# Node pass of a two-layer graph network kernel: where VectorE forms the small products in its step

## The reference

```python
h = maximum(layernorm(x), 0)
x = x + L0(h, edges)          # L0(h) = h + (edge messages summed by dst) @ Wo.T + bo
h = maximum(layernorm(x), 0)
# L1: GCN with self loops, then a two-layer head
h7  = segment_sum((h @ W)[col] * norm, row) + b     # includes the node itself: h * dinv * dinv
out = relu(h7 @ W1 + b1) @ W2 + b2
x = x + out
```

## Time and profile before

| | us |
|---|---|
| median of 3 runs | 1850.17 (1849.44 to 1851.53) |
| the profiled execution, whole | 1868.97 |
| its span, first to last instruction | 1867.3 |
| PE busy in the span | 1629.1 (87%) |
| DVE busy | 1412.2 (76%) |
| POOL busy | 1227.1 (66%) |
| ACT busy | 1119.3 (60%) |

### The profile page before, as it was taken

One profiled execution on the slowest core, in us unless ns is written; L12 is line 12 of the kernel. 1 busy time (PEld: TensorE's weight loads), 2 busy tenths in 40 slices (PEclk: granted clock), 3 DMA queues, 4 the chain that ended last, 5 costly groups with the idle time before them and its releaser, 6 DMA issues.

```text
span 1867.3 us, 29386 instructions
## 1 busy us (share of the span) xinstructions
PE 1629.1 (87%) x6406; PEld 1099.9 (59%) x6406; DVE 1412.2 (76%) x5503; ACT 1119.3 (60%) x2092; POOL 1227.1 (66%) x864
## 2 busy tenths in 40 slices
PE   8788999999999967676675169999999999999998
PEld 4355666666666635454454046666666666666666
DVE  7986777777777639777776497888888888888873
ACT  0155555556666522222222378889889889989984
POOL 3246777777777646888887765666666666666650
PEclk9999999999999987878777679999999999999999
DMA  9997666666666655555556678999999999999981
GB/s 370 419 415 244 175 175 174 174 174 175 177 177 185 195 136 115 118 111 108 113 115 126 136 200 248 255 266 271 269 268 268 267 270 267 267 268 269 274 230 75
DMA packets 148023, 398.67 MB, mean 214 GB/s; under 512 B 20144, under 2 KB 56756, under 8 KB 147974
## 3 DMA queue, kind: packets, MB, share of 16 engines
q1 hardware_dynamic: 89830, 280.18, 43.8%
q0 software_dynamic: 56416, 115.46, 32.8%
q10 hardware_dynamic: 1728, 2.50, 0.4%
HBM read 217.84 MB, written 180.23 MB: 213 GB/s over the span
## 4 chain that ended last, share of the span: by engine, by line
PE 27%; POOL 25%; issue 13%; DMA 11%; DVE 10%; ACT 7%; another core or an unknown queue 4%; SPq 3%; ACTq 0%; DVEq 0%; POOLq 0%
POOL sums_dram L488 9%; DMA out_dram<-cg 8%; PE bank L1361 6%; PE bank L1350 6%; POOL kept L578 6%; PE bank L1246 4%; POOL cg L492 4%; POOL b_rs L484 4%; ACT z L1054 4%; DVE cg L958 3%; PE bank L1178 2%; PE bank L1253 2%; PE bank L1340 2%; SPq L394 1%
## 5 line engine op out<-in xcount | busy, mean ns | idle before, releaser
L1350 PE MATMUL bank<-kept,w 128*128 128x512 f32 x784 | 355.4, 596 | 0.0
L1361 PE MATMUL bank<-w_sb,kept 128*128 128x256 f32 x1568 | 354.3, 379 | 0.0
L578 POOL TENSOR_TENSOR kept<-kept 128x1024 f32<-128x1024 f32 x98 | 232.4, 2371 | 183.4 <-DVE cg L958 183.4
L1361 PEld LDWEIGHTS bank<-w_sb,kept 128*128 128x128 f32 x1568 | 297.9, 190 | 81.9 <-issue 46.4
L488 POOL DMA_INDIRECT sums_dram<-ub,sidx x148 | 244.1, 1649 | 91.3 <-issue 42.3
L1314 PE MATMUL bank<-cg,en 128*128 128x256 f32 x386 | 132.8, 489 | 124.7 <-issue 80.6
L484 POOL TENSOR_TENSOR b_rs<-b_ve,minus_half 128x8 f32<-128x8 f32 x102 | 210.5, 2064 | 28.7 <-DVE b_ve L975 28.7
L1350 PEld LDWEIGHTS bank<-kept,w 128*128 128x128 f32 x784 | 142.6, 192 | 142.3 <-issue 142.3
L1145 ACT ACTIVATE kept<-kept,b_nb,b_rs 128x256 f32<-128x256 f32 x392 | 202.2, 588 | 21.9 <-DVE b_nb L948 21.9
L1246 PE MATMUL bank<-qkv_w,zT 128*128 128x512 f32 x392 | 192.0, 612 | 21.4 <-DVE msg L815 18.0
L1135 ACT ACTIVATE kept<-kept,b_nb,b_rs 128x256 f32<-128x256 f32 x392 | 202.2, 589 | 12.5 <-DVE b_nb L948 12.5
(11 more groups left out here) (172 smaller groups left out, 3260.3 us busy)
## 6 DMA issues: line engine op xcount, KB each, us to landing
sums_dram<-cg SPq DMA_DIRECT2D x196, 512.0 KB
kept<-in_x_dram SPq DMA_DIRECT2D x97, 512.0 KB, 5.7
kept<-sums_dram POOLq DMA_DIRECT2D x97, 512.0 KB, 9.8
cg<-sums_dram SPq DMA_DIRECT2D x97, 512.0 KB, 8.7
out_dram<-cg SPq DMA_DIRECT2D x97, 512.0 KB, 9.8
row_d<-in_dst_dram SPq DMA_DIRECT2D x49, 128.0 KB
row_k<-keys_dram SPq DMA_DIRECT2D x24, 256.0 KB
row_s<-in_src_dram SPq DMA_DIRECT2D x24, 256.0 KB
```

What stands on the lines that cost most here:

```text
L578: pool.tensor_tensor(X1[k.slot(8)], X[k.slot(4)], H[k.slot(2)], ALU.add).then_inc(g_xh, 1)
L1350: ins = pe.matmul(bank[:, 2 + m, :], w01[:, c, m * P:(m + 1) * P], hT[k.slot(2)][:, c * GN:(c + 1) * GN], start=(c == 0), stop=(c == KC - 1))
L1361: ins = pe.matmul(to, rT[k.slot(2)][:, c * GN + j * P:c * GN + (j + 1) * P], w2_sb[:, c, :], start=False, stop=(c == KC - 1), skip_group_c ...
```

## The change

DVE's two small products of step s-1 (with their wait for POOL's roots) leave the head of its step s. They go behind the statistics, aggregates and variances of step s and ahead of `AG`. No instruction is added or dropped, and no other engine's code is touched.

```diff
@@ -938,15 +938,6 @@
             def nodes(s):
                 a, v, r, t = s, s.back(1), s.back(5), s.back(4)
                 z = v.slot(2)
-                if v.within(NG + 4):
-                    dve.wait_ge(g_rs, v.value(1))
-                    if r.within(NG):
-
-                        dve.tensor_tensor(b_rs[z][:, G:2 * G, 0], b_rs[z][:, G:2 * G, 0],
-                                          dinv2[:, bass.ds(r.value(0, G), G)], ALU.mult).then_inc(g_rsd, 1)
-                        dve.wait_ge(g_rsd, r.value(1))
-                    dve.scalar_tensor_tensor(b_nb[z][:, :, :], b_mv[z][:, :, 0:1], -1.0, b_rs[z][:, :, :],
-                                             ALU.mult, ALU.mult).then_inc(g_nb, 1)
                 k = s.back(10)
                 if k.within(NG):
 
@@ -974,6 +965,15 @@
                     dve.wait_ge(g_mv, a.value(1))
                     dve.tensor_scalar(b_ve[a.slot(2)][:, :, :], b_mv[a.slot(2)][:, :, 1:2], EPS, None,
                                       ALU.add).then_inc(g_ve, 1)
+                if v.within(NG + 4):
+                    dve.wait_ge(g_rs, v.value(1))
+                    if r.within(NG):
+
+                        dve.tensor_tensor(b_rs[z][:, G:2 * G, 0], b_rs[z][:, G:2 * G, 0],
+                                          dinv2[:, bass.ds(r.value(0, G), G)], ALU.mult).then_inc(g_rsd, 1)
+                        dve.wait_ge(g_rsd, r.value(1))
+                    dve.scalar_tensor_tensor(b_nb[z][:, :, :], b_mv[z][:, :, 0:1], -1.0, b_rs[z][:, :, :],
+                                             ALU.mult, ALU.mult).then_inc(g_nb, 1)
                 k = s.back(6)
                 if k.within(NG):
                     dve.wait_ge(g_h1, k.value(1))
```

## The result

| | before | changed |
|---|---|---|
| median, us | 1850.59 (1849.44 to 1851.53) | 1964.28 (1961.99 to 1965.17) |
| ratio | 1 | 1.0617 (1.0600 to 1.0633) |
| span of the profiled execution, us | 1867.3 | 1963.5 |

The change costs 113.7 us, 6.2%. The prediction was 1937 us (+87), with a range of 1918 to 1990: the direction and the place were right, the size 27 us short. The measured time lies inside that range, but above the 1918 to 1960 us that the forecast had given itself without a rival.

The account below looks back on a forecast made before the run. PE was taken to bound the node pass at 7.76 us a group. A new loop through M1's banks (+91.7), stalls (0) and the beginning (-5) gave +86.7 us on 1850.2, so 1937 us, range 1918 to 1990.

Parts of the forecast that it names:

- the loop of DVE and POOL: `fin`, X1, DMA issue, roots, small products, next `fin`: 7.74 us, cut by the change, which frees little.
- The loop through M1's banks: `fin`, products, H1, H, rT, M1, M2: 17.57 us per two groups against PE's 7.76 a group, +91.7 us; chance 0.80.
- The unknown term, rT to M1: Hand-over from ACT's rT to PE's first M1 matmul, without a row: taken as 0.15 us, from 0.03 to 0.30.
- The loop before the change: Same loop through M1's banks over three steps: 20.6 us for three groups, 6.9 each, hidden under PE's 7.76.
- The clock: Rival: PE's clock falls in the new idle gaps, 1.7 us lost each time, up to 2012 us; chance 0.11.
- it is little over half: Argument against a clock fall: PE's new gap, 2.05 us per two groups, against the known 3.67 us one.
- every third: Clock rival's milder case: 3.4 us at half clock at every third pair of groups, 1962 us in all.
- The stalls of 8.9 us: All PE stalls from `fin` of group 0 to group 89: left as they are, change 0, from -9 to +9.
- The beginning: Before the first `fin`, later products may miss POOL's X1: -5 us, from -13 to +3.
- The products don't meet X1: Rival denied here: late X1 on POOL holds up L945 by up to 2.13 us, +95, 2032 us; chance 0.03.
- Faster: Rival: rT never the last wait, PE gapless from the first `fin`, -8.9 and -5, 1836 us; chance 0.03.
- no difference: Rival: rT never the last wait, with DVE's code pauses and the beginning as before, 1850 us; chance 0.03.

Follow-up runs that it names:

- experiment 3: Changed kernel with the small products moved directly behind `fin`, ahead of all statistics: 1866.98 us, 0.9988 of the kernel before.
- the early store: Changed kernel with rT ahead of H1 and H on ACT and the store issued one step earlier on SP: 1833.98 us, 0.9911 of the kernel before.
- experiment 1: Changed kernel with the small products moved ahead of the aggregates, behind both groups of statistics: 1891.83 us, 1.0219 of the kernel before.
- experiment 4: Changed kernel with rT ahead of H1 and H on ACT: 1859.80 us, 0.9945 of the kernel before; on a second chip 1843.34 us, 0.9953.
- experiment 6: Changed kernel with each group's PE transposes done twice: 1957.82 us, 1.0469 of the kernel before; on a second chip 1941.49 us, 1.0486.
- experiment 7: Kernel before the change with the store issued one step earlier on SP, nothing else: 1845.68 us, 0.9969 of the kernel before.
- experiment 2: Changed kernel with the small products moved between the statistics of x and those of X1: 1903.92 us, 1.0178 of the kernel before.

## Why the prediction was right, and where it was short

- **What bounds the kernel.** Right: PE had nothing to give, and cutting the loop of DVE and POOL gave nothing in steady state (experiment 3; with the early store too, 693.8 us with the loop cut and 693.2 with it in place). The chain of waits pointed to a loop that was as long as PE's period but was no gain to remove.
- **The loop through M1's banks.** Right in its terms and in its sum of 17.57 us, as measured outside VectorE's loop. Experiments 1 and 4 show it from both sides: shorten it and the time falls by it, take rT from behind the waiting instructions and the loss goes. In the loop of VectorE it is 17.78: 0.2 us a pair, some 8 us in all, weren't in the sum. The unknown term, rT to M1, was 0.14. The loop before the change was reckoned too long: its 7.74 us from `fin` to `fin` already hold the products, which were added once more. By the earlier trace rows the products end 1120.42 - 1113.35 = 7.07 us behind `fin`, so it was 19.5 us for three groups, 6.5 each and not 6.9. It was hidden all the same.
- **The clock.** The forecast gave full clock 0.80 and this rival 0.11; the loop held and the rival came true beside it, at 17 of 44 pairs. The step that failed is the weight put on "it is little over half" of the idle time that was known to lower the clock. Of the idle times of about 2.0 us (1.8 to 2.2), two in five had a stretch at half clock behind them, of those of 0.97 us (experiment 1) none. Worth: 16 more stretches x 1.7 = 27 us, which experiment 6 takes away again. That the rival's price for "every third" pair, 1962 us, is so near to the 1964 measured is in part luck: the 8 us of the loop's small change weren't in it, and about as much was too high in the terms below.
- **The stalls of 8.9 us.** Counted as staying, and laid for a good part to the pause of VectorE's code. That holds: PE's idle time of 3.67 us and the 1.7 us of the half clock behind it are 5.4 of them. Some 3 more are waits for the store (experiment 7), which have room in a longer period. The pause is there in the changed kernel too:

```profile
1135.33 1.22 DVE L949 TENSOR_TENSOR cg<-kept,bank 128x1024 f32<-128x1024 f32 x1 [5.70 <-issue]
```

That some 5 us of the stalls went away in the changed kernel follows from the sum alone (91 for the loop + 8 + 27 = 126, against 121 measured); no run of its own shows it.
- **The beginning.** -5 forecast, -7.5 measured. The reason was half right: of the seven products that met X1 one is left (L975 at 1031.34, 2.31 us), but the variances (now L966) meet it in four steps, with 2.23, 1.59, 1.61 and 1.58 us instead of 0.17. The first of them:

```profile
1049.67 2.34 POOL L578 TENSOR_TENSOR kept<-kept 128x1024 f32<-128x1024 f32 x1 [2.63 <-ACT kept L1145]
1049.80 2.23 DVE L966 TENSOR_SCALAR b_ve<-b_mv 128x8 f32<-128x8 f32 x1
```

- **The other rivals.** The products don't meet X1 in the changed kernel's steady part (L972 0.16 us at the median), though the margin was thinner than reckoned. X1 was to start at most 1.4 us behind `fin`; in every second step it starts 1.92 us behind it (1514.22 and 1516.14 above), held up by H, and ends at 4.3 us, ahead of the products at 4.8. Where the products are moved onto X1 (experiment 2), the price is as computed. "Faster" and "no difference" had no ground.
- **The level.** I took the profiled execution for a longer one of the same kind. By its time and its first edge pass it was one of another chip. As the edge passes carry that difference, the difference forecast didn't suffer.

## What to carry to other kernels

In a software pipeline held together by semaphores, write down each loop that goes over several engines and divide its length by the number of steps it spans. Moving a short instruction later in its own step can take a step out of a loop: here the loop got 2 us shorter, and yet 19.5/3 became 17.57/2. Look behind the waiting instruction on the engine that consumes it: the cost was made by rT, which needed nothing of the products and stood behind those that did, and moving it ahead turned a loss of 114 us into a gain of 9.

## What the runs showed of the hardware that I had not expected

- With an idle time of PE of about 2.0 us in each pair of groups, the granted clock fell to 1.2 GHz 17 times in 44 pairs, nearly always for 3.4 us, and as often in a second trace. With idle times of 0.97 us it fell once, at the pause of VectorE's code, and with 0.29 us never. Filling the idle time with needless transposes gave 27 us back.
- The same program takes 1850 us on one chip and 1869 us on another; the traces have the 19 us in its first edge pass (the second begins at 678.0 and 658.6 us).
- A product of 128x4 elements on VectorE, which takes 0.16 us, was held up by POOL's X1 for 1.2 us at nearly every step of experiment 2. One of 128x8 that started 0.07 us ahead of X1, in experiment 3, wasn't held up.
